# The row sums of a second attention stage: the seventh key tile added on GpSimd instead of multiplied on its own

## The reference, cut to what matters

```
x = x + tanh(g_xattn) * xattn(layernorm(x), ctx_768)      # 8 heads of 64, keys and values from ctx_768
x = x + tanh(g_ffn)   * ffn(layernorm(x))                 # 16 heads of 32, keys and values from x

# in ffn, for every head:
attn = softmax(q_scaled @ k.T / sqrt(32), axis=-1)        # 1024 queries x 1024 keys
h    = attn @ v
# then a gate per token from h, and out = (h * gate) @ Wp.T + bp
```

## Time and profile before

| | |
|---|---|
| median of 3 runs | 5398.33 us (5398.06 to 5402.42) |
| the profiled execution | 5395.54 us, its span 5393.5 us |
| first stage and weights | to about 2300 us of the span |
| second stage, a batch in its middle | about 376 us |
| PE busy | 4848.6 us, 90% of the span |
| POOL busy | 3365.4 us, 62% |
| DVE busy | 3092.1 us, 57% |
| ACT busy | 2605.5 us, 48% |

### The profile page before, as it was taken

The page is one execution under the profiler, slowest core; times in us unless marked ns, Lnnn a source line. Parts: engine busy times, 40 slices in busy tenths (PEclk is TensorE's granted clock), DMA queues, the critical chain, the costliest instruction groups (busy, mean ns, idle before and its releaser), DMA issues.

```text
span 5393.5 us, 67274 instructions
## 1 busy us (share of the span) xinstructions
PE 4848.6 (90%) x21696; PEld 2764.4 (51%) x21696; DVE 3092.1 (57%) x3782; ACT 2605.5 (48%) x4665; POOL 3365.4 (62%) x2676
## 2 busy tenths in 40 slices
PE   1899999999999999969899998998898998889998
PEld 1455555555555556444454464554554554545644
DVE  2464646464546464456766666756757656666653
ACT  2343434343434343425645636646546455456354
POOL 1364646465656465617848747847767578487487
PEclk9899999999999999979999999999999999999999
DMA  8435353534353434141232223132232222222320
GB/s 251 113 83 133 83 133 83 133 83 133 83 133 83 133 83 125 48 119 49 73 87 61 65 81 81 43 99 66 74 84 61 76 76 71 86 61 65 91 51 24
DMA packets 337078, 479.99 MB, mean 89 GB/s; under 512 B 32736, under 2 KB 198112, under 8 KB 336736
## 3 DMA queue, kind: packets, MB, share of 16 engines
q1 hardware_dynamic: 336736, 475.71, 33.5%
HBM read 223.14 MB, written 50.33 MB: 51 GB/s over the span
## 4 chain that ended last, share of the span: by engine, by line
PE 42%; DVE 7%; issue 4%; ACT 2%; POOL 1%; DMA 0%; SPq 0%; ACTq 0%; POOLq 0%; DVEq 0%
PE f_aux L793 13%; PE f_aux L851 9%; PE f_acc L891 8%; PE f_scores L874 7%; DVE f_nm L1147 4%; PE f_aux L903 2%; PE f_aux L912 1%; DVE f_rs L1097 1%; PE f_aux L833 1%; POOL f_added L773 1%; PE f_aux L811 1%; ACT f_probs L1030 1%; SPq L712 0%; ACT f_xs L960 0%; DVE f_st L1092 0%
## 5 line engine op out<-in xcount | busy, mean ns | idle before, releaser
L773 POOL TENSOR_TENSOR f_added<-f_added,f_probs 128x512 f32<-128x512 f32 x1536 | 1921.0, 1294 | 291.4 <-PE f_acc L891 248.4
L1147 DVE TENSOR_REDUCE f_nm<-f_aux 128x1 f32<-128x1024 f32 x1024 | 1224.1, 1220 | 698.4 <-PE f_aux L851 695.8
L773 POOL TENSOR_TENSOR x_added<-x_added,x_probs 128x512 f32<-128x512 f32 x896 | 1127.0, 1293 | 737.2 <-PE x_acc L891 506.4
L1030 ACT ACTIVATE f_probs<-f_scores 128x512 f32<-128x512 f32 x1792 | 968.8, 598 | 569.7 <-PE f_scores L874 518.7
L1147 DVE TENSOR_REDUCE x_nm<-x_aux 128x1 f32<-128x1024 f32 x512 | 619.2, 1222 | 489.3 <-PE x_aux L851 488.6
L874 PE MATMUL f_scores<-f_stack 128*128 128x512 f32 x2048 | 738.5, 431 | 99.7 <-ACT f_probs L1030 92.7
L851 PE MATMUL f_aux<-f_stack 96*128 96x512 f32 x2048 | 697.0, 432 | 113.5 <-DVE f_nm L1147 102.0
L1030 ACT ACTIVATE x_probs<-x_scores 128x512 f32<-128x512 f32 x896 | 500.9, 595 | 510.5 <-PE x_scores L874 488.6
L874 PE MATMUL x_scores<-x_stack 128*128 128x512 f32 x2048 | 615.9, 412 | 4.8 <-ACT x_probs L1030 4.8
L874 PEld LDWEIGHTS f_scores<-f_stack 128*128 128x128 f32 x2048 | 383.6, 195 | 414.9 <-ACT f_probs L1030 168.2
L851 PEld LDWEIGHTS f_aux<-f_stack 96*128 96x128 f32 x2048 | 355.9, 195 | 456.3 <-DVE f_nm L1147 262.0
(11 more groups left out here) (166 smaller groups left out, 5745.2 us busy)
## 6 DMA issues: line engine op xcount, KB each, us to landing
x_wqk<-w_split SPq DMA_DIRECT2D x128, 256.0 KB, 3.5
x_wvo<-w_split SPq DMA_DIRECT2D x32, 1024.0 KB, 9.5
x_stack<-x_cq_hi SPq DMA_DIRECT2D x128, 256.0 KB, 5.0
x_stack<-x_ck_hi SPq DMA_DIRECT2D x128, 256.0 KB, 5.0
f_wqk<-w_split SPq DMA_DIRECT2D x128, 256.0 KB, 3.6
f_wvo<-w_split SPq DMA_DIRECT2D x32, 1024.0 KB, 9.3
f_stack<-f_cq_hi SPq DMA_DIRECT2D x256, 128.0 KB, 2.4
f_stack<-f_ck_hi SPq DMA_DIRECT2D x256, 128.0 KB, 2.4
```

The source lines that it names most:

```text
L773: pool.tensor_tensor(onto, onto, exp_buffer(T, e), ALU.add).then_inc(added_ok, 1)
L1030: act.activation(exp_buffer(T, e), scores[:, u % SCORES, :], ACT.Exp, scale=ph.SCALE).then_inc(probs_ok, 1)
L1147: dve.tensor_reduce(nm[:, e * TT + t:e * TT + t + 1], keys, axis=AX.X, op=ALU.max, negate=True).then_inc(emptied["dve"], 1)
```

## The change

One constant changes:

```
--- before.py
+++ after.py
@@ -48,7 +48,7 @@
         self.SLOTS = 2 if ffn else 4
         self.MROW = 96 if ffn else 64
         self.NP = 10 if ffn else 7
-        self.APART = 1 if ffn else 0
+        self.APART = 0
         self.SUM = 32 if ffn else 64
         self.AT = AT[ffn]
 
```

## The result

The changed kernel takes **5459 us** (median of four runs, 5455 to 5481) against 5400 us of the kernel before beside it on the same chip: ratio 1.0115, 95% interval 1.0085 to 1.0144. That is slower, as forecast, but the forecast was 5426 us: 33 us are missing, more than the forecast's own 28 us of loss. The time lies inside the wide range of 5345 to 5465 us and 4 us outside the forecast's own, 5400 to 5455. The profiled execution took 5460.7 us, with a span of 5458.7 against 5393.5. So the two traces differ by 65 us, and the question is where these lie.

What follows compares the result with a forecast made beforehand. TensorE's products were taken to bound A, C and E to G, GpSimd B and the last batch's end. +1.9 us a batch, times 7 +13, plus 15 for the last batch gave 5426 us; own range 5400 to 5455, wide 5345 to 5465.

Steps and rivals of the forecast that it cites:

- the last batch: End of the last batch, no next batch to fill TensorE: GpSimd's additions run without pause, delaying the end by 15 us.
- A: First half of a second-stage batch, pure TensorE: +4.9 us from value chunks and maxima tiles the new order leaves to it.
- B: Second half of a batch: +1.3 us, its first addition delayed by L760; the new additions themselves cost nothing.
- C: Third half of a batch: -1.1 to -2.2 us, fewer products less some 2.5 us of TensorE stopped by the ring buffer.
- the ring's 2.5 us: First four steps of C: products shorter than GpSimd's additions, so the ring of exponential buffers stops TensorE about 2.5 us.
- D: Fourth half of a batch: +2.5 us, GpSimd 1.3 us later and one addition more in the run L1097 waits out.
- The four small operations at the batch's end: Operations behind L1097 at the batch's end fall among additions: 0 to 4 us on A, taken as 1.5.
- E to G: Fifth to seventh halves together, TensorE-bound: -3.3 us as products fall from 102.7 to 99.3 us; GpSimd just fits.
- H: Eighth half with the batch's end: -2.3 us from fewer products; three value chunks fewer in the end's wait save nothing.
- Rival 1: The lockout of L1097 in D goes: -10 us a batch against the forecast, 5360 us; chance 0.27.
- Rival 3: GpSimd takes over wherever it ran without a gap, lockout longer: near +8 us a batch, 5470 us; chance 0.13.
- Rival 2: TensorE takes all of the gain, the additions disappearing in GpSimd's idle time: 5331 us; chance 0.05.

Runs made afterwards that it cites:

- e2: Changed kernel, its order kept, with the seventh tile's additions run over 16 of 512 columns: 5431 us, ratio 1.0073 to the kernel before.
- e9: New work only in halves A, C, G and H of the first seven batches, order listed anew: 5416 us, ratio 1.0035 to the kernel before.
- e6: Changed kernel with the addition of EPS (L1097) moved from VectorE to ScalarE in the second stage: 5466 us, ratio 1.0132 to the kernel before.
- e11: Changed kernel with the EPS addition on ScalarE and the small operations behind the square root on GpSimd: 5410 us, ratio 1.0013 to the kernel before.
- e3: New order with the old work: short additions as in e2, and both sets of sum products on TensorE again: 5510 us, ratio 1.0224 to the kernel before.
- e5: Kernel before with the addition of EPS (L1097) moved from VectorE to ScalarE in the second stage: 5378 us, ratio 0.9962.

## Why the prediction was right and wrong

**The direction and the last batch** were right, by their mechanism. Halves E, F and G of the last batch have GpSimd busy 36.01 of 36.01, 30.72 of 30.72 and 34.42 of 34.42 us: no pause, as told; the one pause in H, 3.00 us at 5408.12, comes after the sum of G. From the first addition of D to the sum of G it was 5324.22 - 5200.30 = 123.9 us before and is 5388.08 - 5248.34 = 139.7 after, +15.8 for a forecast of 15; A to C, ahead of this, are 4.2 us shorter and what follows the sum is 1.3 longer, so the batch as a whole is 12.9 us longer. In e2, with these additions nearly free, it is as long as before (308.2 us to 308.3). In H of the last batch a VectorE operation on `f_halves` is held for 8.4 us, as none was in the kernel before; e2 has that hold too (8.2 us), and its H there is 68.8 us long, against 68.1 before. The first addition of D and the sum of G:

```profile
5248.34 5.01 POOL L773 TENSOR_TENSOR f_added<-f_added,f_probs 128x512 f32<-128x512 f32 x4 [1.99 <-PE f_acc L891]
...
5388.08 1.70 PE L903 MATMUL f_aux<-f_added,f_ones 128*32 128x512 f32 x8 [3.77 <-POOL f_added L773]
```

**A** was forecast at +4.9 from the products listed into it, and is +5.4; e9 shows the cause, the list, to be right, though a wait is part of its price. **B** +1.3, measured +0.5. **C** -1.1 to -2.2, measured -3.0: the ring's 2.5 us did not come, since e2, without the additions, has the same C. **D** +2.5, measured +0.4: the hold did get longer, by 0 to 0.8 us and not 1.2, and D hardly followed. The four small operations at the batch's end did fall among additions (L1104 went from 3.6 to 9.8 us in all, L1081 from 2.6 to 8.5), but A stayed pure TensorE, so the 1.5 us were nothing. Up to D, with these operations, I had +7.5 (3.5 + 2.5 + 1.5) and 3.3 were measured. The prediction's own terms for A, B and C (+4.9, +1.3, -1.1 to -2.2) add to 4.0 to 5.1, not to the 3.5 that it took, so by its working this miss is larger still. Its sign of L1097 at 9.5 us or more did not come either: 8.3 to 9.1.

**E to G is the step that failed**: forecast -3.3, measured +2.7, so 6 us a batch or 42 in all. The products fell as counted. But they had been counted over the three halves together, with TensorE busy 110 of 115 us, and the new order gave F another list: the sum of E, two rowmax products more and three projection products fewer, in a half where TensorE depends on VectorE's rowmax step by step. The group of the rowmax products in half F, before and then after:

```profile
L851 PE MATMUL f_aux<-f_stack 96*128 96x512 f32 x36 | 11.4, 421 | 1.9 <-DVE f_nm L1147 1.2 <-DMA f_stack<-f_ck_lo 0.8
```

```profile
L851 PE MATMUL f_aux<-f_stack 96*128 96x512 f32 x38 | 13.4, 445 | 3.1 <-DVE f_nm L1147 2.4 <-DMA f_stack<-f_ck_lo 0.7
```

F has 0.8 us more of products, 1.6 us more of TensorE's waits, and its granted clock is 0.96 where it was 1.00; all of this is there without the additions (e2: F 38.60 us, TensorE busy 33.55, clock 0.96) and gone in e9, whose F has the list of before (34.60 us, 31.01, 1.00). So F's list is the cause; whether the sum or the exchanged products weigh more was not tested. E and G gave back only 1.5 us.

**H** was forecast at -2.3 and is +1.6. The value products that left it stood in a stretch that waits for a chain, as the prediction said of three of them; I took the gain for the others all the same. That this is why nothing came back is argued, not tested, and e2 and e6 put H at +0.8.

**Luck.** The sum came as near as it did by errors of both signs: E to H were forecast 9.9 us a batch too short, A to D with the small operations 4.2 us too long. More than half of the forecast loss of 28 us was the last batch, which was right by its mechanism; in a batch in the middle the forecast was +1.9 and the measured loss 7.6, with the one large surprise in F.

**The clock** was in no term. In H of the changed kernel, five windows of 4 us (columns as in the earlier trace rows) show what a pause of TensorE does:

```profile
3904.79:3908.79 4.00, 3.43 (x20) 1.55 (x24) 3.80 (x12) 3.63 (x9) 4.00 (x4) 1.00 0.00 0
3908.79:3912.79 4.00, 1.02 (x9) 0.11 (x8) 3.89 (x5) 1.04 (x3) 4.00 (x4) 1.00 0.00 0
3912.79:3916.79 4.00, 2.23 (x5) 1.82 (x6) 3.97 (x5) 0.58 (x1) 4.00 (x4) 0.63 0.17 66
3916.79:3920.79 4.00, 4.00 (x10) 2.76 (x9) 2.83 (x3) 1.71 (x4) 4.00 (x4) 0.52 0.80 179
3920.79:3924.79 4.00, 4.00 (x22) 2.24 (x21) 1.16 (x3) 0.60 (x1) 3.91 (x4) 1.00 0.49 119
```

TensorE pauses for 4.75 us in the second and third window. In the pause the granted clock falls to its lower level, 1.2 of 2.4 GHz, and stays there for about 7 us (0.63 and 0.52 on the mean of the third and the fourth), and ten instructions fill the 4 us that 22, partly of other shapes, fill afterwards. The sum of length times (1 - granted clock), over windows of a twelfth of a half, is 18.8 us a batch before and 23.3 after, in the last batch 18.7 and 27.3. This counts time in which TensorE had nothing to do as well. Over its busy time alone the sums are 12.6 and 16.4, and 17.9 and 23.7: so the lower clock can have cost 3.8 us of the 7.6 a batch, and over the eight batches 34 us (102 before, 136 after), about half of why TensorE is busy as long as before with 67.5 us less to do. The traces of e2 and e6 have 14.8 and 15.5 us a batch in the same order, so some of it is scatter. In the windows shown the clock falls in TensorE's wait, so I read it as a surcharge on the waits and not as a cause of its own; no run held the clock fixed.

**The rivals.** Rival 1 did not happen (the hold stayed, seven times), but most of its price was sound: 7.7 us a batch in D when e11 takes the hold away, for up to 9 forecast. D to G are then 156 us and not the 149 of GpSimd's own time, since F and G stay at 38.9 and 41.7, and the time falls by 49 us for 66 forecast. The page's rule behind it, from the Trainium skill, "SBUF — State Buffer", "Who interferes with whom", is that the ports are held "for the whole instruction"; here holds of 9 and 11 us through runs of additions of 1.25 us go against reading that as one instruction. Rival 3 named nearly the right sum (5470) with the wrong mechanism: it let GpSimd's work lengthen B, C and D, and e2 shows that in the seven batches it lengthened no half by over 1 us on the mean. Rival 2 did not happen.

## What to carry to other kernels

Where a planner or a sorted list sets the order, an edit is two changes; make the work in the old order and the old work in the new one before you explain a time, and compare by stretch, since here the total alone would have put 59 us down to GpSimd, whose additions cost 13 to 26 of it. The two parts need not add up, so look in each of the kernels for waits that neither the one before nor the one after has. Price a gain only in stretches that TensorE bounds, half by half: products that leave a stretch with waits give nothing back, and those listed into a full one cost all of their time. The instruction that GpSimd held was cured here by giving its work to GpSimd, not by another form of it, nor by taking it away alone, which passed the hold to the next.

## What the runs showed of the hardware

The hold is not bound to one instruction. A tensor_scalar of 4 elements a partition (6.8 to 9.6 us), a tensor_tensor of 4 (6.2 to 9.1) and one of 512 (5.3 to 11.9) were each held to the end of a run of additions on GpSimd, while operations with an input in PSUM took their usual time among such additions (L1130 of the changed kernel 0.69 to 0.70 us, 36 times) and small ones such as L1193 to L1201 waited one addition each. How far into an addition it starts does not decide it: of 46 operations of `f_halves` in all the traces that began 0.6 to 0.7 us into one and waited at all, 39 went with that addition's end and 7, all at the one place in e3, were held to the end of the run; and the held operations on `f_rs` began anywhere from 0.02 to 1.20 us into an addition. What decides stays open. In D the same place is held in all of the seven batches, in each kernel that has an operation of this kind there; in H an operation on `f_halves` is held in all seven batches of e3 and in one batch of e6 (11.9 us), and once in the last batch of the changed kernel and of every kernel in its order. So a small change of work can add a hold or shorten one (e5).
